# A state-space scan layer on one core: half of the weighing of the states moves from VectorE to GpSimd, and the sum over states is made by accumulating transposes

## The reference

```python
x = x + attn(layernorm(x))       # a selective state-space scan
x = x + xattn(layernorm(x), fside, ctx)   # an expert with both matmuls quantised to int8, one per batch
x = x + ffn(layernorm(x), ...)   # gated feed-forward, 704 wide, weights and activations quantised

# attn, with b=4, l=256, d=256, n=16 states
u = depthwise_conv(x, 4 taps) + conv_b
dt, Bm, Cm = split(u @ xproj.T)                       # 128, 16, 16
delta = softplus(dt @ dtproj.T + dtproj_b)
h[t] = exp(delta[t] * A) * h[t-1] + delta[t] * Bm[t] * u[t]      # for each channel and state
y[t] = sum over n of h[t, n] * Cm[t, n]
attn = y + u * D_skip
```

## Time and profile before

| | |
|---|---|
| median of 3 runs | 250.36 us (250.27 to 250.86) |
| the profiled execution, its own time | 251.69 us |
| its span, first to last instruction | 249.9 us |
| busy in the span: VectorE | 220.4 us, 88% |
| TensorE / ScalarE / GpSimd | 168.8 / 144.7 / 144.6 us |
| mean granted TensorE clock | 0.888 of full speed |

### The profile page before, as it was taken

The page is one execution under the profiler, slowest core; times in us unless marked ns, Lnnn a source line. Parts: engine busy times, 40 slices in busy tenths (PEclk is TensorE's granted clock), DMA queues, the critical chain, the costliest instruction groups (busy, mean ns, idle before and its releaser), DMA issues.

```text
span 249.9 us, 2858 instructions
## 1 busy us (share of the span) xinstructions
PE 168.8 (68%) x676; PEld 98.6 (39%) x676; DVE 220.4 (88%) x419; ACT 144.7 (58%) x307; POOL 144.6 (58%) x174
## 2 busy tenths in 40 slices
PE   0187498898485497867577479649878768729434
PEld 0155364464141344443423335234545446415232
DVE  2759989999999989989999999989899997894861
ACT  4018537965859375675566787346456886535151
POOL 3540898485456499457599564761484827551442
PEclk9999689999959769799999999776999997975957
DMA  6985643365353234352354644000000000000003
GB/s 179 341 298 104 230 135 109 110 138 116 84 127 113 98 114 138 127 129 77 90 155 148 152 98 129 0 0 0 1 3 1 21 0 0 25 0 0 0 0 126
DMA packets 15103, 23.23 MB, mean 93 GB/s; under 512 B 1136, under 2 KB 6640, under 8 KB 15088
## 3 DMA queue, kind: packets, MB, share of 16 engines
q1 hardware_dynamic: 13792, 21.92, 30.7%
q10 hardware_dynamic: 1296, 1.15, 1.4%
HBM read 21.88 MB, written 1.18 MB: 92 GB/s over the span
## 4 chain that ended last, share of the span: by engine, by line
DVE 35%; issue 22%; PE 19%; ACT 7%; POOL 7%; DMA 5%; SPq 2%; POOLq 0%; DVEq 0%; ACTq 0%
DVE Q L1043 8%; PE pY L741 6%; DVE prod L1054 6%; DMA fs_t<-w_in_t 5%; PE Q L229 3%; DVE am L980 3%; PE Q L893 3%; PE pA L708 2%; DVE w L1212 2%; POOL drive L354 2%; DVE tf L1219 2%; POOL w L384 2%; PE pX L229 2%; PE pA L229 1%; ACT Q L498 1%
## 5 line engine op out<-in xcount | busy, mean ns | idle before, releaser
L354 POOL TENSOR_TENSOR drive<-du,bc 128x512 f32<-128x512 f32 x64 | 79.9, 1272 | 31.2 <-DVE Q L1043 27.0
L741 PE MATMUL pY<-prod,ident 128*128 128x512 f32 x128 | 69.1, 678 | 12.7 <-DVE prod L1054 7.5
L1043 DVE TENSOR_TENSOR_SCAN Q<-Q,drive 128x512 f32<-128x512 f32 x64 | 75.1, 1212 | 0.8 <-ACT Q L498 0.8
L498 ACT ACTIVATE Q<-delta,negA 128x255 f32<-128x255 f32 x128 | 54.8, 470 | 24.9 <-DVE Q L1043 24.4
L1054 DVE TENSOR_TENSOR prod<-Q,bc 128x512 f32<-128x512 f32 x64 | 41.2, 674 | 0.9 <-PE pY L741 0.9
L741 PEld LDWEIGHTS pY<-prod,ident 128*128 128x128 f32 x128 | 25.5, 215 | 41.0 <-issue 27.9
L384 POOL TENSOR_TENSOR w<-w 128x352 f32<-128x352 f32 x16 | 15.4, 974 | 12.4 <-DVE w L1212 12.3
L229 PE MATMUL Q<-ident,w 128*128 128x128 f32 x48 | 10.1, 374 | 14.0 <-ACT w L597 14.0
L301 POOL TENSOR_SCALAR ve<-mv 128x2 f32<-128x2 f32 x12 | 3.9, 325 | 25.0 <-DVE mv L971 24.9
L1212 DVE TENSOR_TENSOR w<-Q,ws 128x704 f32<-128x704 f32 x16 | 13.6, 880 | 0.8 <-PE Q L877 0.5
L229 PEld LDWEIGHTS Q<-ident,w 128*128 128x128 f32 x48 | 7.6, 191 | 16.1 <-ACT w L597 15.8
(11 more groups left out here) (154 smaller groups left out, 330.3 us busy)
## 6 DMA issues: line engine op xcount, KB each, us to landing
bc<-bc_dram SPq DMA_DIRECT2D x32, 512.0 KB, 4.8
w<-w_gate_up SPq DMA_DIRECT2D x1, 1408.0 KB, 9.6
x_sb<-x SPq DMA_DIRECT2D x4, 256.0 KB, 3.6
fs_t<-w_in_t SPq DMA_DIRECT2D x1, 1024.0 KB, 12.4
out<-x_sb ACTq DMA_DIRECT2D x8, 128.0 KB, 1.8
w<-w_down SPq DMA_DIRECT2D x1, 704.0 KB, 11.0
ctx_t<-w_out_t SPq DMA_DIRECT2D x1, 512.0 KB, 12.7
xproj<-xproj_t SPq DMA_DIRECT2D x1, 160.0 KB, 3.0
```

The source lines that it names most:

```text
L354: pool.tensor_tensor(drive[:, s % 2, h], du[:, b, h].unsqueeze(1).to_broadcast([P, SPS, T]), bc[:, g % 4, 0].rearrange("p (n t) -> p n t", ...
L498: act.activation(decay[:, h, n, 1:T], delta[:, b, h, 1:T], ACT.Exp, scale=negA[:, h, k:k + 1]).then_inc(S["decay_ready"], 1)
L741: ins = pe.matmul(pY[:], ident[:], prod[:, s % 2, :, n, :], start=(s == 0 and n == 0), stop=False, skip_group_check=True)
L1043: dve.tensor_tensor_scan(hid[:, h].rearrange("p n t -> p (n t)"), decay[:, h].rearrange("p n t -> p (n t)"), drive[:, s % 2, h].rearrange( ...
```

## The change

- `weigh` is split. VectorE weighs half 0 as before, GpSimd half 1. For that the scan of half 1 writes to a new SBUF tensor `hid_sb` of two buffers in place of a PSUM bank. The semaphore `weighed` becomes `weighed0` (VectorE) and `weighed1` (GpSimd), and who waited for one waits for both, where it concerns both.
- `sum_step` takes each 128 x 128 block of `prod` as the stationary operand and the identity as the moving one, in transpose mode, and accumulates in PSUM: y arrives with positions on partitions, as x has them. That is 8 matmuls of 128 columns a step in place of 2 of 512. `skip_y` becomes 4 matmuls of 128 columns in place of 2 of 256. `out_y` and `turn_y` are gone, and `residual1` reads `pY`.
- All five lists of calls are written anew. VectorE's now rounds six pieces of the feed-forward weights ahead of the first scan, and looks for the maxima of `fs_t` inside the scan phase.

```diff
+        hid_sb = sb("hid_sb", [P, 2, SPS * T])
-        y_sb = sb("y_sb", [P, H, T])
-        pY = psum("pY", [P, H, T])
+        pY = psum("pY", [P, JT, D])
-        hid = Q[:, 2:4].rearrange("p h (n t) -> p h n t", n=SPS)
+        hid = Q[:, 2]
...
                     sp.wait_ge(S["drive_ready"], H * (g - 3))
-                    sp.wait_ge(S["weighed"], H * (g - 3))
+                    sp.wait_ge(S["weighed0"], g - 3)
+                    sp.wait_ge(S["weighed1"], g - 3)
...
+            def weigh(b, s):                    # GpSimd
+                g = STEPS * b + s
+                pool.wait_ge(S["scanned"], H * g + 2)
+                if g >= 2:
+                    pool.wait_ge(S["summed"], g - 1)
+                pool.tensor_tensor(prod[:, s % 2, 1].rearrange("p n t -> p (n t)"), hid_sb[:, s % 2], bc[:, g % 4, 1], ALU.mult)\
+                    .then_inc(S["weighed1"], 1)
...
-            def out_y(b):
-                act.wait_ge(S["y_skip"], b + 1)
-                act.activation(y_sb[:], pY[:], ACT.Copy).then_inc(S["y_ready"], 1)
...
             def sum_step(b, s):
-                pe.wait_ge(S["weighed"], H * (g + 1))
+                pe.wait_ge(S["weighed0"], g + 1)
+                pe.wait_ge(S["weighed1"], g + 1)
                 if s == 0 and b > 0:
-                    pe.wait_ge(S["y_ready"], b)
+                    pe.wait_ge(S["x1_ready"], b)
                 for n in range(SPS):
-                    ins = pe.matmul(pY[:], ident[:], prod[:, s % 2, :, n, :], start=(s == 0 and n == 0),
-                                    stop=False, skip_group_check=True)
+                    for h in range(H):
+                        for j in range(JT):
+                            ins = pe.matmul(pY[:, j, h * P:(h + 1) * P], prod[:, s % 2, h, n, j * P:(j + 1) * P], ident[:],
+                                            start=(s + n + h + j == 0), stop=False, is_transpose=True, skip_group_check=True)
...
             def scan(b, s, h):
-                if u >= 2:
-                    dve.wait_ge(S["weighed"], u - 1)
-                dve.tensor_tensor_scan(hid[:, h].rearrange("p n t -> p (n t)"),
+                if h == 0 and g >= 1:
+                    dve.wait_ge(S["weighed0"], g)
+                if h == 1 and g >= 2:
+                    dve.wait_ge(S["weighed1"], g - 1)
+                dve.tensor_tensor_scan(hid_sb[:, s % 2] if h else hid,
...
             def residual1(b):
-                dve.wait_ge(S["y_turned"], b + 1)
-                dve.tensor_tensor(x_sb[:, b], x_sb[:, b], pA[:, 0].rearrange("p (j d) -> p j d", j=JT), ALU.add).then_inc(S["x1_ready"], 1)
+                dve.wait_ge(S["y_skip"], b + 1)
+                dve.tensor_tensor(x_sb[:, b], x_sb[:, b], pY[:], ALU.add).then_inc(S["x1_ready"], 1)
```

More of the change, by code:

```diff
@@ L423, in _ @@
+            final(3, 1)
         @block.scalar
@@ L678, in _ @@
+            unmagic4(2, 0); unmagic4(2, 1); quant3(3); unmagic3(3); tanh3(3, 0); tanh3(3, 1); quant4(3, 0)
+            quant4(3, 1); store_out(0, 1); store_out(1, 0); store_out(1, 1); unmagic4(3, 0); unmagic4(3, 1)
+            store_out(2, 0); store_out(2, 1); store_out(3, 0); store_out(3, 1)
         @block.tensor
@@ L747, in skip_y @@
                 for h in range(H):
-                    ins = pe.matmul(pY[:, h], cdiag[:, h, TAPS], u_t[:, b, h], start=False, stop=(h == H - 1), skip_group_check=True)
+                    for j in range(JT):
+                        ins = pe.matmul(pY[:, j, h * P:(h + 1) * P], u_t[:, b, h, j * P:(j + 1) * P], cdiag[:, h, TAPS],
+                                        start=False, stop=(h == H - 1), skip_group_check=True)
                 ins.then_inc(S["y_skip"], 1)
-            def turn_y(b):
-                pe.wait_ge(S["y_ready"], b + 1)
-                if b > 0:
-                    pe.wait_ge(S["xbc_ready"], b)
-                else:
-                    prep_banks_free(NB - 1)
-                for j in range(JT):
-                    for h in range(H):
-                        ins = turn(pe, pA[:, 0, j * D + h * P:j * D + (h + 1) * P], y_sb[:, h, j * P:(j + 1) * P])
-                ins.then_inc(S["y_turned"], 1)
             def turn_y2(b):
@@ L765, in turn_y2 @@
                     pe.wait_ge(S["gu_ready"], 2 * b)
+                else:
+                    prep_banks_free(NB - 1)
                 for h in range(H):
@@ L782, in back1x @@
                 pe.wait_ge(S["xs_ready"], H * (b + 1))
-                pe.wait_ge(S["x1_ready"], b + 1)
+                if b > 0:
+                    pe.wait_ge(S["xbc_ready"], b)
+                else:
+                    prep_banks_free(NB - 1)
                 for j in range(JT):
@@ new lines, in _ @@
+            wmax_in(2); wmax_in(3); weigh(0, 7); scan(1, 0, 0); weigh(1, 0); scan(1, 0, 1); scan(1, 1, 0)
+            scan(1, 1, 1); weigh(1, 1); residual1(0); scan(1, 2, 0); scan(1, 2, 1); stats2(0); prep_relu(2)
+            weigh(1, 2); scan(1, 3, 0); scan(1, 3, 1); round_w1(9); weigh(1, 3); scan(1, 4, 0); scan(1, 4, 1)
+            prep_relu(3); weigh(1, 4); wmax_ctx(0); wmax_ctx(1); prep_bc(3); prep_delta(2); prep_delta(3)
+            wmax_inv(); scan(1, 5, 0); scan(1, 5, 1); norm2(0); amax_x(0); ratio_x(0); weigh(1, 5); scan(1, 6, 0)
```

277 lines of the change are left out of this document (132 added, 145 removed).

## The result

The changed kernel takes **256.48 us** (median of 4 runs, 254.67 to 257.96) against 250.51 us: ratio 1.023, 95% interval 1.017 to 1.030. On another chip it took 257.44 us against 249.87 (1.025 to 1.035). The forecast was 248.0 us, its outer range 242.5 to 253.5: the kernel got slower where it was to get faster. The profiled execution took 256.85 us, with a span 4.8 us longer than before. Intervals rest on a kernel's faster executions, and the traces of experiments 2, 8, 11, 13 (with fifteen, and with eight as first placed) and of the repeated run in 1 come from executions 1.5 to 2.4% above their kernel's fastest, so their landmarks are used with that margin.

What follows compares the result with a forecast made beforehand. VectorE's sum was taken to bound the scan phase, GpSimd's after the change. Scan phase -3.2, tail +0.6 and +0.3 gave -2.3 us: 248.0 us from 250.36, own range 245.5 to 249.6, 8-in-10 range 242.5 to 253.5.

Steps and rivals of the forecast that it cites:

- What bounds it now: Scan phase before the change: bound by the sum of VectorE's instructions, busy 142.0 of 145.5 us.
- GpSimd's sum: Scan phase from GpSimd's second step to its last drive: 130.2 us of work, weighings costing what drives do.
- The stalls: Scan phase, beyond GpSimd's sum: 4 us exclusion, 2 us late loads, 3 us waits, putting the last scan at 170.1 us.
- the rival of two engines in turn: Scan phase: VectorE and GpSimd wait for each other; 15 us of stalls give 254.1 us; chance of slower 0.27.
- Late loads: Scan phase: loads of B and C, now waiting for GpSimd's weighing four steps back, cost GpSimd 2 us.
- waits for scans: Scan phase: GpSimd waits for scans, sums and small results at more places, 3 us including TensorE.
- Exclusion: Scan phase: VectorE operations with two SBUF operands and GpSimd block each other, costing GpSimd 4 us.
- VectorE costed at 120 us, and 12.2 us to be won: Scan phase: VectorE's need falls from 142.0 to about 120 us; GpSimd becomes the bound, limiting the gain to 12.2 us.
- The tail at +0.6 and +0.3: After the last scan: 0.6 us lost before the first product, 0.3 us at the end, same operations between.
- TensorE at nothing: Step sums by transposes, 1.3 or 2.1 us a step, free TensorE time; costed at nothing, without cover a gain.
- The rival by the clock: Scan phase: transposes lower TensorE's clock, the expert's chain comes 2 to 3 us later, no change at 250.4 us; chance 0.06.
- The exclusion rule: VectorE instructions with two SBUF inputs contend with GpSimd, the second to issue fully blocking; those with at most one don't.

Runs made afterwards that it cites:

- experiments 2: Changed kernel with each step's sum made by plain matmuls with the identity instead of transposes: 259.05 us, ratio 1.034.
- 8: Changed kernel with two PSUM buffers for half 0's states, its weighing behind both scans at eight steps: 256.15 us (1.012 to 1.024).
- 11: Changed kernel with VectorE's 32 weighings cut to 16 of 512 columns, so y is wrong: 253.93 us.
- 13: Kernel before with accumulating transposes, some half 1 weighings moved to GpSimd: fifteen 264.43 us, eight 260.18 us, eight placed one step earlier 254.54 us.
- 1: Kernel before with only the sums changed to accumulating transposes, all weighing on VectorE: 248.74 us, ratio 0.995; repeated with more rounds 249.81 us, ratio 0.996.
- 15: Kernel before with accumulating transposes, ScalarE instead of VectorE making `z_pos` of batches 1 to 3: 250.48 us, ratio 1.000.
- experiment 5: Changed kernel with six buffers for B and C in place of four: 261.13 us (1.039 to 1.052).
- 7: Changed kernel with the fourth batch's normalisation wholly on GpSimd and one weight rounding ahead of the first scan: 256.15 us (1.015 to 1.029).
- 10: Changed kernel with GpSimd's 32 weighings cut to 16 of 512 columns, so y is wrong: 247.03 us.
- 9: Changed kernel with GpSimd's last two weighings moved ahead of the expert's residual of batch 1: 256.47 us (1.013 to 1.032).
- experiment 3: Changed kernel with two unused filler matmuls on TensorE behind each sum of steps 0 to 29: 255.93 us, ratio 1.025.

## Why the prediction was wrong

In the traces the forecast of 2.3 us less missed by 7.1 us: 3.2 in the scan phase (170.1 forecast, 173.3 measured) and 3.9 in the tail (0.9 forecast, 4.8 measured). The other 1.4 us lie between the profiled executions and the medians. The direction was wrong, too.

**What bounds it now: right, but read too far.** VectorE at 142.0 of 145.5 us bounds the scan phase. Yet two attempts to take 2.6 us and 4.7 us off it with the old lists gained nothing (experiments 13 and 15).

**GpSimd's sum: right.** Forecast 130.2 us, measured 130.0 in the window [28.90, 171.90]. A weighing takes a drive's time, and the scan into SBUF kept its length (1.20 us). GpSimd does set the pace for part of the way: cutting its weighings moves the last scan by 7 us, cutting VectorE's by nothing.

**The stalls: the term that failed in the phase.** I took 9 us; they are 13.0, above the 11.3 us from which the rival of two engines in turn was to decide. By that rival's own sum they make 250.4 + 13.0 - 11.3 = 252.1 us; what lies above it is the tail's. With a start 0.65 us earlier, 161.1 - 0.65 + 13.0 = 173.4 us, as measured. Late loads were 4.2 us (forecast 2), waits for scans 7.7 (forecast 3 with TensorE's). Exclusion I had put on GpSimd at 4 us; on GpSimd it is small (1.2 us at 82.81), and on VectorE it grew by 5.8 us, which the forecast's 120 us left out. Of the 4.0 us of dependent neighbours some 2 count as busy. These make 8 of the 12.6 us by which VectorE's 132.6 us exceed the 120; the rest is not traced.

The three stalls were not terms to be added. Load waits removed come back as blocked VectorE (experiment 5), blocked instructions removed as others blocked (7), neighbours parted as waits for decays (8, in the one trace taken). GpSimd and VectorE are each busy for over 90% of the phase, with one decay and two drives per half between them. What an experiment takes out in one place, waits in another filled. That this is so because of the few buffers is argued; no run has more buffers for drive or decay.

**VectorE costed at 120 us, and 12.2 us to be won: wrong.** With GpSimd's weighings nearly free, VectorE still needs 127.2 us and idles 11.3; only 7 us were there with these lists.

**The tail at +0.6 and +0.3: the step that failed most, 4.8 us in place of 0.9.** "What comes behind is the same set of operations" is true, and says nothing of when. I compared the first product (178.4 before, 178.6 after: the 0.6 us were not even needed) and stopped there. Up to the second batch's first product 4.0 us more were lost (19.8 us in place of 15.9). Old lists in the tail shorten this stretch to 18.6 us, with the rounding early to 16.7, but the first product comes later, by 2.6 and 4.0 us. Two things stand behind the 4.0 us, and the runs divide them only roughly. One is the lists: VectorE has 1.8 us more work ahead of that product, and even at a clock of 0.92 the stretch takes 17.8 us. The other is TensorE's clock, 0.83 there in place of 1.00, which the forecast had not looked at in the tail: 0.9 us with the old lists, and up to 2 us with the new ones, where the kernels compared differ in more than the clock. GpSimd's two late weighings are not the cause: with them cut (10) the stretch is still 19.9 us, and with them moved (9) it is 18.3 us only because the first product comes 1.3 us later. Which link holds the rest stays open.

**TensorE at nothing: right in sign, the size off.** A step's sum takes 1.04 us at full clock and 1.92 at half by the timeline; forecast 1.3 and 2.1.

**The rival by the clock.** The clock fell as the Trainium skill, page TensorE: Matmul & The Clock Gate, Part 4, would have it for transposes: 0.89 to 0.75 in the phase, and 0.80 with the transposes alone. What it costs in the phase is small as far as the runs show: experiment 1 isn't slower and experiment 3 moved no scan, though between the two traces of experiment 1 the phase is 3.2 us longer at the lower clock. In the tail it takes part in the 4.0 us, as said above. Within the repeated run of the transposes alone the time goes with the clock all the same: three executions at 0.829 to 0.837 took 247.2 to 248.5 us, three at 0.788 to 0.795 250.2 to 250.9. Which causes which no run here shows; fillers on that kernel were not tried.

**The exclusion rule.** The Trainium skill, page SBUF — State Buffer, section Who interferes with whom, has the first to issue hold the shared ports "for the whole instruction". The words stand there with VectorE's modes that use both ports, which the section says `tensor_scalar` can enter; the forecast left this exception out. By its reading a normalisation, with one SBUF tensor as input, would be free; those in the earlier trace rows and at 49.17 were blocked. Which mode they ran in no run shows. The traces show more than one instruction's wait, but not always: up to four GpSimd instructions in a row went by, 4.99 us, while in the changed kernel the same operation came through at the seam of two that followed each other without a pause:

```profile
86.95 1.35 DVE L983 TENSOR_SCALAR y<-x_sb,mv,rstd 128x256 f32<-128x256 f32 x1
86.89 2.54 POOL L345 TENSOR_TENSOR du<-delta,u_t 128x512 f32<-128x512 f32 x2
```

What decides between the two is open. I had taken half of one instruction.

## What to carry to other kernels

An engine's slack isn't room for work that stands in the loop of the bounding engine: of GpSimd's 49 us of slack eight weighings used 10, and the kernel got 5 us slower. Where two engines would both be over 90% busy with one or two buffers between them, take all stalls as one quantity, and expect a fix to surface elsewhere. Cut the moved work to almost nothing on the chip first: here that gave 247.0 us, only 3 us less than the 249.8 us without any move, and there is no reason to hope for more from the move itself in these lists. Follow a tail past its first landmark to the one from which the rest runs at nearly constant length, and read the granted clock in each stretch of it, not only its mean.

## What the hardware showed unexpectedly

- A VectorE `TENSOR_SCALAR` with SBUF operands waited through a run of GpSimd instructions until GpSimd had a gap: 2.56 us over two, 4.99 us over four, for 0.40 us of work. Another, of 0.40 us as well, came through after one (1.35 us), without a gap.
- Dependent neighbours on VectorE cost 0.15 us (scan, then its weighing) and 0.22 us (weighing, then the scan into its buffer), and the timeline marks no idle time there.
- Accumulating transposes in float32 worked as a sum over states and take 1.04 us for eight at full clock; a plain sum of 1024 columns took 1.88 us.
